# The slots' root mean square in the recurrent stage: one wide product of ones and ScalarE's Ln and Exp in place of narrow products, GpSimd's power and a spread by identity

## The reference, cut to what matters

```
sn     = slots * rsqrt(mean(slots*slots, axis=-1) + 1e-6) * w_slot
scores = einsum('bkd,bmd->bkm', sn @ Wq.T, k_proj) * D**-0.5      # D = 256
attn   = softmax(scores, axis=-2)                                 # over the slots k
attn   = attn / (sum(attn, axis=-1) + 1e-6)
slots  = gru_cell(einsum('bkm,bmd->bkd', attn, v_proj), slots, ...)
```

## Time and profile before

| | |
|---|---|
| median of three runs | 1197.67 us |
| the profiled execution's own time | 1196.42 us |
| its span | 1194.6 us |
| mean granted TensorE clock | 0.958 |
| TensorE busy | 88% of the span |
| VectorE, ScalarE, GpSimd busy | 62%, 35%, 29% |

### The profile page before, as it was taken

One profiled execution on the slowest core, in us unless ns is written; L12 is line 12 of the kernel. 1 busy time (PEld: TensorE's weight loads), 2 busy tenths in 40 slices (PEclk: granted clock), 3 DMA queues, 4 the chain that ended last, 5 costly groups with the idle time before them and its releaser, 6 DMA issues.

```text
span 1194.6 us, 17670 instructions
## 1 busy us (share of the span) xinstructions
PE 1050.8 (88%) x5946; PEld 859.4 (72%) x5946; DVE 742.4 (62%) x1821; ACT 422.6 (35%) x791; POOL 351.3 (29%) x293
## 2 busy tenths in 40 slices
PE   7899989999886886999999999999997399999990
PEld 5557767478465774778888888888885189998990
DVE  5566754774744666666666767556657466666664
ACT  2213132050414653434433445444442243333330
POOL 2505145041233442001111101110242734536510
PEclk9999999999988998899999999999998799999995
DMA  9001025000055565001000000000010685527216
GB/s 334 22 0 36 1 72 160 0 1 1 23 177 177 163 209 188 1 1 36 1 1 1 1 1 1 1 1 1 19 51 32 235 265 157 166 74 241 78 54 229
DMA packets 73267, 95.84 MB, mean 80 GB/s; under 512 B 6128, under 2 KB 59632, under 8 KB 73072
## 3 DMA queue, kind: packets, MB, share of 16 engines
q1 hardware_dynamic: 58576, 65.35, 17.1%
q0 software_dynamic: 14624, 29.64, 7.7%
HBM read 66.23 MB, written 28.74 MB: 79 GB/s over the span
## 4 chain that ended last, share of the span: by engine, by line
PE 48%; DVE 17%; another core or an unknown queue 13%; issue 7%; ACT 5%; DMA 4%; SPq 3%; POOL 3%; DVEq 0%; ACTq 0%; POOLq 0%
PE PS L205 13%; PE PS L207 12%; PE PS L206 12%; PE PS L1739 2%; PE PS L1624 2%; PE PS L1827 2%; PE PS L1711 2%; POOL rstd L941 2%; DMA S<-routed 1%; ACT PH L1138 1%; DVE hs L683 1%; PE PS L1834 1%; DVE act L704 1%; DVE st L1206 1%
## 5 line engine op out<-in xcount | busy, mean ns | idle before, releaser
L941 POOL TENSOR_TENSOR rstd<-ve,minus_half 128x4 f32<-128x4 f32 x40 | 45.3, 1132 | 349.5 <-DVE ve L1213 229.4
L580 POOL DMA_INDIRECT results<-S,place_of x80 | 77.6, 970 | 186.1 <-DVE S L728 102.2
L205 PE MATMUL PS<-xt,split 128*128 128x256 f32 x312 | 89.4, 287 | 10.8 <-issue 7.7
L206 PE MATMUL PS<-xt,split 128*128 128x256 f32 x312 | 88.2, 283 | 0.0
L207 PE MATMUL PS<-xt,split 128*128 128x256 f32 x312 | 88.2, 283 | 0.0
L948 POOL DMA_INDIRECT routed<-S,dest x64 | 65.2, 1019 | 60.7 <-DVE dest L1316 43.4
L653 ACT ACTIVATE act<-PS,colv 128x256 f32<-128x256 f32 x84 | 39.8, 474 | 119.1 <-PE PS L207 91.6
L1630 PE MATMUL PS<-ones_bf 128*128 128x512 bf16 x200 | 57.1, 439 | 19.1 <-DMA routed<-S,dest 13.7
L205 PEld LDWEIGHTS PS<-xt,split 128*128 128x128 f32 x312 | 59.7, 191 | 13.2 <-issue 9.7
L205 PE MATMUL PS<-split,hs 128*128 128x256 f32 x184 | 59.6, 324 | 5.6 <-DVE hs L683 2.9
L704 DVE SCALAR_TENSOR_TENSOR act<-PS,colv,act 128x256 f32<-128x256 f32 x84 | 40.6, 484 | 37.8 <-ACT act L653 31.4
(11 more groups left out here) (348 smaller groups left out, 3124.2 us busy)
## 6 DMA issues: line engine op xcount, KB each, us to landing
S<-routed SPq DMA_DIRECT2D x44, 264.0 KB, 2.8
HB<-results SPq DMA_DIRECT2D x12, 512.0 KB, 6.6
routed<-blank SPq DMA_DIRECT2D x20, 264.0 KB
raw<-gate_w SPq DMA_DIRECT2D x8, 512.0 KB
raw<-up_w SPq DMA_DIRECT2D x8, 512.0 KB
raw<-down_w SPq DMA_DIRECT2D x8, 512.0 KB
X<-x SPq DMA_DIRECT2D x4, 512.0 KB
raw<-m_w SPq DMA_DIRECT2D x8, 256.0 KB
```

The lines of the kernel that those rows point to most:

```text
L205: pe.matmul(out_, a[1], b[0], start=first, stop=False)
L206: pe.matmul(out_, a[0], b[1], start=False, stop=False)
L580: pool.indirect_dma_start(out=results[m], out_offset=bass.IndirectOffsetOnAxis(ap=place_of[:, i, a:a + 1], axis=0), in_=moe[m].y[:, i, a], ...
L941: pool.tensor_tensor(rstd[h][:], ve[h][:], minus_half[:], ALU.pow).then_inc(sem(name), 1)
```

## The change

The squares of the two column halves are added first by VectorE (new stage `sqs`), then one product with a 128 x 128 matrix of ones both sums over the partitions and leaves the row of 512 on all partitions (`ss`). ScalarE takes Ln with scale 1/256 and 1e-6 as bias, then Exp with scale -0.5, in the row's place. The stages `ve` (VectorE and GpSimd) and `rsb` are gone, the factor -1/16 goes into VectorE's multiplication (line 1534, now with a scalar). In ScalarE's list `-na` moves from between `rs` and `expA` to behind `phB` and what follows it. `hi` and `lo` are not changed; `sqs` stands ahead of `lo`.

```diff
@@ ORDER_C, the steps' lists (cut to the places that differ)
     "pe":
-    12:final2 !6,7:ss -na 6,7:ss 8:lt0 9:lt1 !6,7:rsb !6,7:scores 0:kk1 -za 6,7:rsb 6,7:scores -hb
+    12:final2 !6,7:ss -na 6,7:ss 8:lt0 9:lt1 !6,7:scores 0:kk1 -za 6,7:scores -hb
     "act":
-    sq hi -ra 8:lt0 9:lt1 6:pv2 7:pv3 rs -na expA phA expB phB 0:kk1 0:pv1 8:exp0 9:exp1 -za -hb
+    sq hi -ra 8:lt0 9:lt1 6:pv2 7:pv3 rs expA phA expB phB 0:kk1 0:pv1 8:exp0 9:exp1 -na -za -hb
     "dve":
-    6:slotT2 7:slotT3 lo ve 0:combine1 -ga
+    6:slotT2 7:slotT3 sqs lo 0:combine1 -ga
     "pool":
-    6:final0 7:final1 ve 0:slotsA1
+    6:final0 7:final1 0:slotsA1
@@ ScalarE
                 elif stage == "rs":
-                    act.wait_ge(sem("rsb_ps"), q + 1)
-                    act.activation(root_rows(h), bank(h, 3), ACT.Copy, scale=-1.0 / 16).then_inc(sem("root_rows"), 1)
+                    act.wait_ge(sem("ss_ps"), q + 1)
...
+                    act.activation(root_rows(h), bank(h, 3), ACT.Ln, bias=slot_eps[:, 0:1], scale=1.0 / D).then_inc(sem("root_rows"), 1)
+                    act.wait_ge(sem("root_rows"), 2 * q + 1)
+                    act.activation(root_rows(h), root_rows(h), ACT.Exp, scale=-0.5).then_inc(sem("root_rows"), 1)
@@ VectorE
-                elif stage == "ve":
-
-                    dve.wait_ge(sem("ss_ps"), q + 1)
-                    dve.tensor_scalar(ve[h][:], bank(h, 2)[:, 0:TT], 1.0 / D, 1e-6, ALU.mult, ALU.add).then_inc(sem("var_ready"), 1)
+                elif stage == "sqs":
+                    dve.wait_ge(sem("slot_sq"), 2 * q + 1)
+                    dve.tensor_tensor(squares(h)[:, 0], squares(h)[:, 0], squares(h)[:, 1], ALU.add).then_inc(sem("slot_sq"), 1)
                 elif stage in ("mulA", "mulB"):
...
-                    dve.wait_ge(sem("root_rows"), q + 1)
+                    dve.wait_ge(sem("root_rows"), 2 * q + 2)
...
-                        step(dve.tensor_tensor(scaled(h, j), bank(h, j), root_rows(h), ALU.mult))
+                        step(dve.scalar_tensor_tensor(out=scaled(h, j), in0=bank(h, j), scalar=-1.0 / 16, in1=root_rows(h), op0=ALU.mult, op1=ALU.mult))
@@ TensorE
-                    pe.wait_ge(sem("slot_sq"), q + 1)
-                    for j in range(TT):
-                        for c in range(C):
-                            ins = pe.matmul(bank(h, 2)[:, j:j + 1], squares(h)[:, c, j * P:(j + 1) * P], ones[:, 0:1], start=c == 0, stop=c == C - 1)
-                    ins.then_inc(sem("ss_ps"), 1)
-                elif stage == "rsb":
                     if q == 0:
                         spin(bank(1, 3), 6)
-                    pe.wait_ge(sem("root"), q + 1)
-                    for j in range(TT):
-                        ins = pe.matmul(bank(h, 3)[:, j * P:(j + 1) * P], rstd[h][:, j:j + 1].to_broadcast([P, P]), ident[:], start=True, stop=True)
-                    ins.then_inc(sem("rsb_ps"), 1)
+                    pe.wait_ge(sem("slot_sq"), 2 * q + 2)
+                    pe.matmul(bank(h, 3), ones[:], squares(h)[:, 0], start=True, stop=True).then_inc(sem("ss_ps"), 1)
                 elif stage == "scores":
...
                         if j == TT - 1:
-                            pe.wait_ge(sem("root_rows"), q + 1)
+                            pe.wait_ge(sem("root_rows"), 2 * q + 1)
```

More of the change, by code:

```diff
@@ L129, in build @@
         minus_half = sb("minus_half", [P, TT])
+        slot_eps = sb("slot_eps", [P, 1])
         hbq = sb("hbq", [P, C])
@@ L912, in _ @@
         def _(pool):
+            pool.memset(slot_eps[:], 1e-6).then_inc(sem("slot_eps"), 1)
             pool.memset(blank[:], 0.0).then_inc(sem("blank"), 1)
@@ L935, in _, with power @@
             ln = [0]
-            def power(h, name="rstd_ready"):
+            def power(h):
                 ln[0] += 1
                 pool.wait_ge(sem("var_ready"), ln[0])
-                pool.tensor_tensor(rstd[h][:], ve[h][:], minus_half[:], ALU.pow).then_inc(sem(name), 1)
+                pool.tensor_tensor(rstd[h][:], ve[h][:], minus_half[:], ALU.pow).then_inc(sem("rstd_ready"), 1)
             def scatter(m, n, h, tiles_of=range(TT)):
@@ L1007, in _ @@
                     power(h)
-                elif stage == "ve":
-                    power(h, "root")
                 elif stage == "weights":
@@ L1147, in _ @@
                 elif stage == "rs":
-                    act.wait_ge(sem("rsb_ps"), q + 1)
-                    act.activation(root_rows(h), bank(h, 3), ACT.Copy, scale=-1.0 / 16).then_inc(sem("root_rows"), 1)
+                    act.wait_ge(sem("ss_ps"), q + 1)
+                    if q == 0:
+                        act.wait_ge(sem("slot_eps"), 1)
+                    if it == 1 and n >= 2:
+                        act.wait_ge(sem("logits_t"), B + n - 1)
+                    act.activation(root_rows(h), bank(h, 3), ACT.Ln, bias=slot_eps[:, 0:1], scale=1.0 / D).then_inc(sem("root_rows"), 1)
+                    act.wait_ge(sem("root_rows"), 2 * q + 1)
+                    act.activation(root_rows(h), root_rows(h), ACT.Exp, scale=-0.5).then_inc(sem("root_rows"), 1)
                 elif stage in ("expA", "expB"):
```

## The result

| | time | before, on the same chip | ratio, 95% interval |
|---|---|---|---|
| changed kernel | 1189.7 us (median, 1187.4 to 1190.8) | 1197.8 us | 0.9929 [0.9917, 0.9941] |
| once more, later | 1190.6 us | 1196.8 us | 0.9947 [0.9929, 0.9965] |

A forecast was written before the change was run, and what follows sets the result against it. TensorE, busy 410.03 of 425 us, was taken to set the stage's time. Root -21.6 plus 10.0 for delays gave -11.6 us: 1184.8 from the profiled 1196.4, 1186 as median; range 1181 to 1207, the forecast's own 1181 to 1193.

The forecast's parts named there:

- Table placement: ScalarE: 24 table loads either way; ahead of Ln, and then ahead of either the row's Exp or the moved Tanh.
- the first way: Exp is taken from Tanh's table set: loads ahead of Ln and ahead of the first Exp, none later; leaned to.
- TensorE, root: TensorE from ra to scores: 2.6 to 2.7 us in place of 4.47, 1.8 a step, 21.6 over twelve steps.
- a mis-sized gain: Sign of a wrong forecast: TensorE waits over 0.5 us for the sum of squares, where 0.2 was put.
- the clock might dip less: TensorE's clock, 0.98 over the stage, might dip less without the narrow sums: part of the lower bound, 1181 us.
- The row: ScalarE's Ln and Exp in place of Copy: in time or 0.8 us late, some 0.15 us a step staying.
- The Tanh's move: VectorE's -za and division start 1.3 us later; TensorE idles 7.8 us in six steps, 1.2 in step 10: 9.0.
- The clock: TensorE's clock at the late turns: the forecast counted no falls in gaps of 2.2 us.
- Rival 2: Clock falls in the forecast's own gaps, five at 1.4 us: 1193 us, about no change; chance 0.18.
- Rivals 1 and 3: Load ahead of the moved Tanh, 1203.4 us, chance 0.27; load costing over 1.28 us, 1207 or 1212, chance 0.08.
- rival 1: A table load between phB and the moved Tanh makes -za 2.7 us late: 1203.4 us, slower; chance 0.27.
- Rival 4: One table set has all three functions, so no loads: 0.15 us a step better, 1185 us; chance 0.03.

The follow-up runs named there:

- e1: The changed kernel with the Tanh (-na) put back between rs and expA, so the new root alone: 1172.6 us, ratio 0.9824 to the kernel before.
- e2: The kernel before with only the Tanh (-na) moved as in the changed kernel: 1204.8 us, ratio 1.0089 to the kernel before.
- e3: The changed kernel with Identity in place of Ln, so no table loads in the stage (result not the root): 1183.1 us, ratio 0.9911.
- e4: The changed kernel with eight idle TensorE products ahead of the turn in steps 2 to 5 and 9: 1179.3 us, ratio 0.9867.
- e5: The changed kernel with an unused one-column Ln ahead of the moved Tanh, adding two table loads there: 1224.0 us, ratio 1.0248.
- e6: e1 with the scores' wait for VectorE's tokens' choice moved from first to second group: 1171.9 us, ratio 0.9788 to the kernel before.

## Why the prediction was right, and where its sum was off

*Table placement.* This was the one question that no row settled, and the lean to the first way held: 12 loads ahead of Ln, 12 ahead of the row's Exp, none at the Tanh. The ground given, a load placed for the instruction that uses it, is consistent with that and no more. The Trainium skill (ScalarE activation tables: per-element evaluation and per-set limits, Table sets in the compiler and the runtime) says that the loads are placed per block by the greedy longest run. Taken over the whole step, that would have put Ln and Exp into one set; here Exp got its own load 0.02 us behind Ln, and where the blocks end no trace shows. The drain of about 1.38 us that the Trainium skill (ScalarE: Activation LUTs, What ACT_TABLE_LOAD costs) adds to a switch is not in this trace either: in step 3 Tanh ends at 577.76, the load stands from 577.77 to 579.05 and Ln starts at 579.07.

*TensorE, root.* 1.8 us a step forecast, 2.01 measured (e1), 2.12 from the products in step 3. What was mis-sized is small: the wide product and `na` together were put at 2.3 to 2.5 and took 2.35, the wait for the sum of squares at 0.2 and it is shorter. The twelve steps are not alike, though. Step 0 gave far more, 4.05: it has no gates to hide the trip and runs at 1.2 GHz, where the sixteen records of the narrow products took 3.54 us. Step 7 gave 1.16 (39.10 to 37.94), waiting 0.87 for the sum of squares (more than the 0.5 that was to count as a mis-sized gain), and 8 and 9 gave 0.93 each, as the old spread had hidden the 0.84 us of waiting for tokens' choice. Step 6 waits as long as 7 and gave 2.7 (43.50 to 40.79 from the scores of step 5 to its own) for a reason that nobody forecast: in the trace of before the clock falls there behind the narrow sums, with TensorE at work but for 0.17 us ahead of them (columns as in the earlier trace rows).

```profile
690.00:692.00 2.00, 2.00 (x15) 1.82 (x15) 0.90 (x3) 0.00 (x0) 0.69 (x1) 1.00 0.00 0
692.00:694.00 2.00, 2.00 (x7) 1.59 (x6) 1.69 (x2) 0.00 (x0) 0.69 (x1) 0.55 0.00 0
```

e2, which keeps the narrow sums, has such a fall in steps 6 and 7, and none of the nine traces with the wide product has one between sum and scores, step 0 apart, which starts at 1.2 GHz. That fits the prediction's remark that the clock might dip less with the narrow sums gone; that they are the cause isn't shown, since the other steps have them and keep the clock. In total e1 gained 21.0 us by its ratio; 21.6 less 0.15 a step were forecast. The total is right because these deviations cancel, and so by luck in part.

*The row.* 0.8 us late forecast, 0.64 measured (first multiplication at S + 2.38 in place of S + 1.74), and 0.03 a step of it left instead of 0.15 (e3).

*The Tanh's move.* 9.0 us forecast as the wait that grows ahead of the turns, 9.0 to 9.2 found in TensorE's waits (8.2 to 17.2), of which 0.4 in step 9 come with the root and stand in e1 too. Every link came as written: `-za` 1.19 later against 1.3, division S + 18.21, turn 2.0 after the last product that it follows.

*The clock.* This is the step that was off. Rival 2 took five falls of 1.4 us, at a chance of 0.18, and the forecast none. Four came (2, 3, 5, 9), at 1.5 to 1.6 each by e4: 6 us. So -21.0 for the root, +9.0 for the waits and +6 for the clock are -6, against the -6.3 and -8.2 of the runs. The time is nearer to rival 2's 1193 than to 1186 by the second measurement, and midway by the first. That the fall needed a gap as long as 2.92 us was never stated by a row; 2.0 us was enough, not always. The time lies in the range of 1181 to 1193 because its upper end had room for five. The prediction placed 2.2 us "nearer the latter" of its two known points and still gave the falls too little weight.

*Rivals 1 and 3* fell with the placement: no load at the Tanh, and the load costs ScalarE nothing outside of its own 1.28 us. e5 shows that rival 1's mechanism is real where loads stand there. *Rival 4*, no loads, would differ by 0.03 us a step (e3).

**Open.** Why a 2.0 us gap keeps the clock in one step and loses it in the next: steps 3 and 4 differ by 0.06 us in the gap and nothing that the trace shows sets them apart, and e2 kept it in all of steps 2 to 5, where its turns wait 1.99 to 2.06 us, and lost it in step 9 at 1.99. Whether one table set for Ln and Exp could be had, and what it would do, wasn't tried. The sum of the parts for the changed kernel, -6, is made of a ratio and of single traces, and is no closer than the 2 us between its two measurements.

## What to carry to other kernels

Judge a bundle by its halves: here one half was worth 21 us and the other cost 11 to 15, and the version without the second (e1, or e6 with a wait moved) beats both kernels, 1172 us. When an instruction of one engine is moved down its queue, follow it to the engine that waits last, and price two things there: the idle time itself, and the clock that TensorE may lose in it, here 1.5 us where it fell at a gap of 2 us, more than the 1.3 us of delay that had opened it. A table load in time in which ScalarE waits anyway cost nothing that could be measured here, the same load in front of an operand that others wait for costs its length and what follows.

## What the runs showed of the hardware

- The same idle gap of TensorE, 2.00 to 2.06 us, kept the granted clock at 2.4 GHz in one step and saw it go to 1.2 in another, and in a second execution of the same kernel the steps that lost it were others, four of five both times (the fifth, of step 9, 2.4 us long, lost it twice); with gaps of 1.98 to 2.07 us e3 lost it in three of five and e2 in one. After a gap of 4.9 us the loss was dearer, 2.4 us against 1.5. After one of 4.19 us, ahead of step 1's turn, the step took 35.8 us in both executions of the changed kernel and 36.65 in e4.
- The clock fell once to 1.2 GHz without idle time but 0.17 us, behind the narrow products of step 6 (0.55 in the window 692 to 694 of the kernel before), and twice in e2.
- A switch of tables in this stage costs ScalarE 1.28 us and nothing that the trace shows beside it; the activation behind it starts 0.02 us later.
- A full-precision product 512 columns wide holds TensorE's queue for 0.57 us until the next product starts, and the six products behind it take 1.78 us in place of the 1.39 that six take elsewhere: nearly 1 us in all, as costed, but only 0.57 of it until the next product starts. A second one directly behind it, in the same sum, added 0.74 and 0.6 to the step.
